# Tile statistics a phase ahead of their transposes, row sums one half step later, inverses widened by TensorE, the value bias on ScalarE

## What is computed

```
x = x + squared(layernorm(x))   # softmax-free: attn = (q k)^2, masked, divided by its row sum + eps
x = x + gated(layernorm(x))     # one shared head of keys and values picked for each token by argmax of a gate
x = x + mqa(layernorm(x))       # 16 heads of queries, one head of keys and values, biases on all products
x = x + gated(layernorm(x))
```

## Time and profile before

| | |
|---|---|
| median of 3 runs | 4368.68 us (4368.31 to 4374.84) |
| the profiled execution | 4371.04 us, of which its span is 4369.3 us |
| TensorE matmul busy | 3769.0 us (86%) |
| GpSimd busy | 2965.8 us (68%) |
| VectorE busy | 1880.1 us (43%) |
| ScalarE busy | 1638.2 us (37%) |
| mean granted TensorE clock | 0.953 |

### The profile page before, as it was taken

How to read it: one execution, slowest core, us unless ns; L and a number is a source line. 1 busy time by engine, 2 the same in 40 slices (tenths; PEclk the granted TensorE clock), 3 DMA queues, 4 the chain that set the end, 5 groups by cost and what they waited for, 6 DMA issues and landing times. The chain is left out here.

```text
span 4369.3 us, 67371 instructions
## 1 busy us (share of the span) xinstructions
PE 3769.0 (86%) x26082; PEld 1520.9 (35%) x26082; DVE 1880.1 (43%) x4874; ACT 1638.2 (37%) x2433; POOL 2965.8 (68%) x2207
## 2 busy tenths in 40 slices
PE   7898998986989899898878878888898898998986
PEld 5343434332433333333333332333333333333332
DVE  1222222222555455455454444444454455555552
ACT  1544544552143333333434333333323333333343
POOL 2888787894076766767777666675565657666687
PEclk8999999998999999999999999999999999999998
DMA  1000100012010100101010010000100101000001
GB/s 68 15 15 22 37 20 30 11 59 73 10 30 1 59 1 23 37 1 40 20 32 28 11 37 13 27 32 15 44 1 15 44 1 59 1 23 27 1 29 40
DMA packets 63385, 115.08 MB, mean 26 GB/s; under 512 B 8673, under 2 KB 9185, under 8 KB 63073
## 3 DMA queue, kind: packets, MB, share of 16 engines
q1 hardware_dynamic: 63072, 110.77, 7.9%
HBM read 77.19 MB, written 33.55 MB: 25 GB/s over the span
## 5 line engine op out<-in xcount | busy, mean ns | idle before, releaser
L866 ACT ACTIVATE probs_soft<-banks 128x1024 f32<-128x1024 f32 (+1 forms) x960 | 848.3, 935 | 1339.8 <-PE banks L1171 1335.4
L774 POOL TENSOR_TENSOR added_soft<-added_soft,probs_soft 128x512 f32<-128x512 f32 (+1 forms) x380 | 1151.8, 3031 | 18.5 <-POOL added_soft L767 3.2
L959 DVE CUSTOM_DVE_ANT_0 banks<-banks,mask 128x128 f32<-128x128 f32 (+3 forms) x1536 | 701.3, 527 | 682.9 <-PE banks L1186 682.9
L954 DVE TENSOR_REDUCE maxima_soft<-banks 128x2 f32<-128x1024 f32 x384 | 452.4, 1221 | 503.3 <-PE banks L1186 503.3
L751 POOL TENSOR_SCALAR_AFFINE_SELECT probs_soft<-probs_soft 128x512 f32<-128x512 f32 x384 | 239.1, 635 | 568.6 <-ACT probs_soft L866 568.3
L1186 PE MATMUL banks<-k_soft,q_soft 32*128 32x512 f32 (+3 forms) x4608 | 508.8, 534 | 64.1 <-ACT probs_soft L866 63.6
L1139 PE MATMUL banks<-wide,xnT_soft 128*128 128x512 f32 x1024 | 500.6, 612 | 19.3 <-DVE picking_soft L938 11.0
L872 ACT ACTIVATE probs_squared<-banks,key_scale_squared 128x512 f32<-128x512 f32 (+3 forms) x768 | 378.9, 588 | 287.3 <-PE banks L1171 282.5
L1171 PE MATMUL banks<-q_soft,k_soft 32*128 32x512 f32 (+3 forms) x4608 | 481.2, 500 | 0.0
L1232 PE MATMUL banks<-probs_soft,v_soft 128*32 128x512 f32 (+3 forms) x4608 | 446.2, 507 | 10.2 <-DVE scaled_out_soft L1083 3.5
L774 POOL TENSOR_TENSOR added_squared<-added_squared,probs_squared 128x512 f32<-128x512 f32 (+1 forms) x124 | 376.9, 3039 | 5.1 <-POOL added_squared L774 1.4
(11 more groups left out here) (152 smaller groups left out, 4271.3 us busy)
## 6 DMA issues: line engine op xcount, KB each, us to landing
tiles_soft<-out SPq DMA_DIRECT2D x96, 256.0 KB, 2.7
rest_soft<-out SPq DMA_DIRECT2D x96, 256.0 KB, 2.9
out<-rest_soft SPq DMA_DIRECT2D x96, 256.0 KB, 2.1
tiles_squared<-in_x SPq DMA_DIRECT2D x32, 256.0 KB, 2.7
rest_squared<-in_x SPq DMA_DIRECT2D x32, 256.0 KB, 2.9
out<-rest_squared SPq DMA_DIRECT2D x32, 256.0 KB, 2.0
wide<-in_gated_wqkvT SPq DMA_DIRECT2D x3, 1024.0 KB, 7.7
raw_wq<-in_squared_wq SPq DMA_DIRECT2D x1, 1024.0 KB, 5.6
```

The costliest lines, as they stand in the source:

```text
L774: ins = pool.tensor_tensor(sums, sums, slot(ph, n)[:, :, col:col + width], ALU.add)
L866: ins = act.activation(slot(ph, n)[:, 2 * a:2 * a + 2, 0:width], score_pair(e, a)[:, :, 0:width], ACT.Exp, scale=SCALE)
L954: ins = dve.reduce_max(m["maxima"][:, ph % 2, 2 * a:2 * a + 2, t, p], score_pair(e, a)[:, :, col:col + width], AX_X)
L959: ins = dve.tensor_tensor_reduce(scores, scores, k["mask"][:, CHUNK - width:CHUNK], 1.0, MASKED, ALU.add, ALU.max, m["maxima"][:, ph % 2, ...
```

## The change

- `norm_events` and `plan`: the `stats` of a stage's first 4 tiles move from the second phase of the stage before (right ahead of the first `ln`) to its first or second phase, sprinkled over that phase's other work (`sprinkled`). The `stats` of tiles 4 to 7 come one `ln` earlier. At most one `ln` goes into a half step, with `due` letting an output that is not due be passed over. The first four `rload` of a stage move to the head of its first phase.
- `SUMS_AT` goes from (15, 9) to (16, 10): `sm` now stands behind the `keys` burst that followed it. `rs` keeps its place, since its distance falls from 2 to 1, and `rw` as well. `nrm` moves with `sm`. The output tiles of the second token half get an earliest half step.
- `widen` goes. `rw` reads the 16 reciprocals directly: 16 matmuls (4 tiles, 4 heads), whose stationary is one column read 32 times, with the identity as moving operand.
- `scaled_out` has 4 buffers in place of 2.
- The value bias is a per-partition bias in ScalarE's copy of `v_parts`; VectorE's addition and the semaphore for it go.

```diff
+SCALED = 4
-SUMS_AT = (15, 9)
+SUMS_AT = (16, 10)
...
         steps.append([("ln", s, t)] + [("load", s, t + TILES)] * (t + TILES < NT))
-        if t >= 2 and t + 2 < NT:
-            steps[-1].append(("stats", s, t + 2))
+        if t and t + 3 < NT:
+            steps[-1].append(("stats", s, t + 3))
...
+def sprinkled(work, some):
+
+    placed, first = list(work), len(work) // 3
+    for n in reversed(range(len(some))):
+        placed.insert(first + (len(work) - first) * n // len(some), some[n])
+    return placed
...
     if kind == "gated":
-        return [(("rs", ph, c), 2)]
+        return [(("rs", ph, c), 1)]
     if kind == "mqa":
-        return [(("rs", ph, c), 2), (("widen", ph, c), 3), (("rw", ph, c), 4)]
+        return [(("rs", ph, c), 1), (("rw", ph, c), 3)]
...
+    if event[0] == "out" and event[2] >= TPC:
+        return SUMS_AT[1] + 4
...
+def due(queue, n):
+
+    for x, (e, first, _) in enumerate(queue):
+        if first <= n:
+            return x
+        if "out" not in (e[0], e[1][0] if e[0] == "more" else ""):
+            return None
+    return None
...
+        head = ([("rload", s - 1, t) for t in range(TILES)] * (s > 0) + head[0], head[1])
...
-            work = [(head[0], 1), (parted(own[0]), HALVES - 2), (mixed(parted(outs[:half]), parted(own[1]), kinds), 2 * HALVES - 2)]
+            work = [(head[0], 1), (sprinkled(parted(own[0]), head[1]), HALVES - 2), (mixed(parted(outs[:half]), parted(own[1]), kinds), 2 * HALVES - 2)]
...
-        work += [(head[1], 2 * HALVES - 2), (parted(merged), 2 * HALVES + 6), (parted(later + first), (3 if kinds[s + 1:s + 2] != ["squared"] else NG) * HALVES - 2),
+        work += [(parted(merged), 2 * HALVES + 6), (parted(later + first), (3 if kinds[s + 1:s + 2] != ["squared"] else NG) * HALVES - 2),
...
-                elif u == "widen":
-                    wait_free(pool, ("rs", *e[1:]))
-                    if place[e]:
-                        wait_work(pool, ("rw", *order["widen"][place[e] - 1][1:]))
-                    pool.tensor_copy(m["wide_inverse"][:], m["few_inverse"][:, :, :, None].broadcast_to([P, TPC, HG, D]))\
-                        .then_inc(sg.widened, 1)
...
-                    take_out(e, m["v_parts"][:, e[2]], work[:, bank(e), :])
+                    take_out(e, m["v_parts"][:, e[2]], work[:, bank(e), :], weights["mqa"]["bv"][:, 0:1])
...
-                        if n >= 2:
-                            dve.wait_ge(sg.summed, n - 1)
+                        if n >= SCALED:
+                            dve.wait_ge(sg.summed, n - SCALED + 1)
...
-                    pe.wait_ge(sg.widened, place["widen", ph, c] + 1)
+                    need(("rs", ph, c))
                     for t in range(TPC):
-                        ins = pe.transpose(tile_of(out, t), m["wide_inverse"][:, t].rearrange("p i d -> p (i d)"), k["ident"][:])
+                        for i in range(HG):
+                            ins = pe.matmul(tile_of(out[D * i:D * i + D, :], t), m["few_inverse"][:, t, i:i + 1].broadcast_to([P, D]), k["ident"][:],
+                                            start=True, stop=True)
```

More of the change, by code:

```diff
@@ L318, in plan @@
         if s:
-            outs = [("rload", s - 1, t) for t in range(TILES)] + [e for t in range(NT) for e in
-                                                                 [("out", s - 1, t)] + [("rload", s - 1, t + TILES)] * (t + TILES < NT)]
+            outs = [e for t in range(NT) for e in [("out", s - 1, t)] + [("rload", s - 1, t + TILES)] * (t + TILES < NT)]
         half = next((n for n, e in enumerate(outs) if e == ("out", s - 1, TPC)), 0)
@@ L342, in plan @@
             own = [features(4 * s + 2), features(4 * s + 3)]
-            work = [(head[0], 1), (mixed(parted(outs[:half]), parted(own[0]), kinds), 2 * HALVES - 2), (parted(own[1]), 3 * HALVES - 2)]
+            work = [(head[0], 1), (sprinkled(mixed(parted(outs[:half]), parted(own[0]), kinds), head[1]), 2 * HALVES - 2), (parted(own[1]), 3 * HALVES - 2)]
             if s == stages - 1:
@@ L587, in act_program @@
     order = {name: [e for e in events if e[0] == name] for name in
-             ("load", "rload", "stats", "out", "mxr", "split", "krep", "vst", "ksq", "qsq", "kvar", "nrm", "rs", "widen", "rw", "gate")}
+             ("load", "rload", "stats", "out", "mxr", "split", "krep", "vst", "ksq", "qsq", "kvar", "nrm", "rs", "rw", "gate")}
     order["picks"] = [e for e in events if e[0] in ("kall", "vall")]
@@ L830, in _ @@
                         pool.wait_ge(sg.rest_in[t % TILES], loads)
-                        pool.tensor_tensor(x, x, m["scaled_out"][:, n % 2, :], ALU.add).then_inc(sg.summed, 1)
+                        pool.tensor_tensor(x, x, m["scaled_out"][:, n % SCALED, :], ALU.add).then_inc(sg.summed, 1)
                 elif u == "rload" and kind_of(e[1]) == "mqa":
@@ L1023, in _ @@
                     ins.then_inc(sg.work_free[bank(e)], 1)
-                    wait_free(dve, e)
-                    dve.tensor_tensor(out, out, weights["mqa"]["bv"][:, None, :].broadcast_to([P, TPC, D]), ALU.add)\
-                        .then_inc(sg.biased_values, 1)
                 elif u == "v2":
@@ L1065, in _ @@
                         if n:
-                            dve.wait_ge(sg.widened, n)
+                            wait_work(dve, order["rw"][n - 1])
                         dve.reciprocal(m["few_inverse"][:], columns).then_inc(sg.work_free[bank(e)], 1)
@@ L1221, in _ @@
                         else:
-                            pe.wait_ge(sg.biased_values, place["vst", s, NC - 1] + 1)
+                            for half in range(NC):
+                                need(("vst", s, half))
                     if not soft:
```

26 lines of the change are left out of this document (14 added, 12 removed).

## The result

The changed kernel takes 4149.66 us (median of 4 runs, 4142.34 to 4152.43) against 4368.57 us for the kernel before, measured beside it. The medians differ by 219 us. The forecast was 4147 us, in a range of 4085 to 4250.

What follows compares the result with a forecast made beforehand. TensorE's work plus 600 us without a matmul bounds it. 4371.0 - 110 (tiles) - 53 (inverses) - 55 (sums) - 50 (clock) + 26 (inverse matmuls) + 20 (collisions) = 4149, so 4147 as median; 8-in-10 range 4085 to 4250.

Steps and rivals of the forecast that it cites:

- What bounds it: Whole kernel: time is TensorE's own work plus its waits, 600 us without a matmul.
- Tiles: TensorE's waits for GpSimd's normalized tiles: first four normalized a phase earlier, gain 110 of 120.1 us.
- The worry: Tiles 4 to 7: load to stats becomes one ln shorter, so 10 us of the gain is left out.
- Inverses: TensorE's waits at rw for widened inverses: 56.8 us becomes 4, gain 53; the 16 matmuls cost 26 us.
- Sums: Row sums waiting for ScalarE's copy of a value part: gain 57.9 us, less 3; counted as 55.
- Clock: Half-clock stretches at tile and inverse waits: 59 us comes back, 50 taken; mean clock to about 0.975.
- Collisions: Moved work on VectorE and GpSimd, and TensorE arriving earlier at exponentials and maxima: nothing to 60 us, 20 taken.
- The bound for being wrong: TensorE's waits for exponentials and maxima: forecast is wrong if they grow by more than 60 us.
- Array drains: Rival: sums between score bursts change the array's shape twice more each, costing 35 us: 4182; chance 0.12.
- Handed over: Rival: half of tile and inverse waits return at other releasers, collisions 30 us larger: 4284; 4215 to 4350, chance 0.17.
- Serial inverses: Rival: the 32 records at rw don't overlap, 0.194 us each, 147 us more than counted: 4294; chance 0.04.
- VectorE's queue: Rival: earlier stats of tiles 4 to 7 hold up maxima, 4.5 us per tile, slower at 4399; chance 0.03.

Runs made afterwards that it cites:

- run with the late tiles back: Changed kernel with only the statistics of tiles 4 to 7 back one step later: 4170.83 us, ratio 0.9544.
- sums alone: Kernel before with only the row sums moved to (16, 10) and widening one step behind rs: 4317.01 us, ratio 0.9880.
- sums undone: Changed kernel with the row sums back at the half steps (15, 9): 4202.73 us, ratio 0.9608.
- inverses alone: Kernel before with only the inverses read directly by 16 matmuls, without widen: 4301.72 us, ratio 0.9845.
- two buffers: Changed kernel with 2 buffers for scaled_out in place of 4: 4148.56 us, ratio 0.9488.
- two buffers, inverses undone: Changed kernel with 2 scaled_out buffers and with widen and the 4 transposes per inverse put back: 4194.87 us, ratio 0.9593.
- tiles alone: Changed kernel with row sums and widen as before and two scaled_out buffers, leaving the tiles' part and value bias: 4255.30 us, ratio 0.9735.
- tiles undone: Changed kernel with the statistics of all tiles back where they were: 4255.24 us, ratio 0.9734.
- doubled run: Changed kernel with the 16 matmuls that read the inverses issued twice, same result written again: 4173.88 us, ratio 0.9546.

## Why the prediction held, step by step

**What bounds it.** The reading that the time is TensorE's work plus its waits held: 195.8 of the 218.6 us came from time without a matmul. By the forecast's own terms that was 110 + 53 + 55 - 20 = 198. The matmuls were to lose 50 - 26 = 24 us, and lost 22.8.

**Tiles.** Forecast 110, of 120.1 us to be had. The wait itself fell by 153.9 - 39.3 = 114.6 us, since only 5.8 us and not 10 were left outside the openings. Undoing the part costs 106 us and having it alone saves 114, both with what it does to the clock. The worry was right in kind, that the later tiles would take something back, and VectorE's wait for tiles did grow, from 40.0 to 50.1 us. The changed kernel's two groups of statistics:

```profile
L993 DVE BATCH_NORM_STATS2 stats_soft<-tiles_soft 128x6 f32<-128x512 f32 x96 | 65.5, 683 | 38.0 <-DMA tiles_soft<-out 38.0
L993 DVE BATCH_NORM_STATS2 stats_squared<-tiles_squared 128x6 f32<-128x512 f32 x32 | 21.9, 685 | 12.1 <-DMA tiles_squared<-in_x 12.1
```

The forecast would be wrong "if VectorE waits for tiles by more than 40 us"; since 40.0 us were there already, this is read as growth, and 10 came. The run with the late tiles back shows that they were not on TensorE's path.

**Inverses.** The gain in waits was right, 52.0 us for a forecast of 53. The cost was the term that was mis-sized: 26 us by 0.05 us per record, from the nearest row of the same shape. Measured were 0.034 us per record, and 0.024 to 0.027 for the second set of them. Against the transposes that is 34.6 - 24.8 = 9.8 us. But the transposes stood behind long waits: 10.3 of their 24.8 us lie in stretches at half clock, and none of the 34.6. At full clock they would have been an estimated 24.8 - 10.3 / 2 = 19.6 us, and the replacement costs 15.0. The forecast had this part of the clock's gain twice, in the 24.8 and in the 59 us of its clock term. The nearest row had 8 records. Of the 0.4 us of so short a group, 273 ns are the length of a single record. In 32 records in a row (1.08 us at 2581.76) each one's share is smaller.

**Sums.** Forecast 55 us. The sums had 57.9 us of waits for a copy of `y`. They have none now, and 2.0 us for other banks (L1213). Undone and alone, the move is worth 53 us each. What was to be late next, the copy of the sums behind two exponentials, is there with 10.2 us in 25 waits of L1323. It was not foreseen that the gated division would then be late for the bank: 17.5 + 11.3 us at L1152 and L1348. The timeline of the changed kernel about 1585 us has such a case:

```profile
1584.66 0.19 DVE L984 TENSOR_REDUCE minus_max_soft<-maxima_soft 128x16 f32<-128x32 f32 x1
1584.77 0.25 DVE L1074 RECIPROCAL inverse_soft<-banks 128x16 f32<-128x16 f32 x1
...
1585.07 1.12 PE L1152 MATMUL banks<-wide,xnT_soft 128*128 128x512 f32 x2 [2.15 <-DVE inverse_soft L1074]
```

The reciprocal, 0.25 us long, stands in VectorE's queue behind a burst's maxima and their reduction, and the projection that wants its bank waits 2.15 us. The 17.5 us are not all new, for they stand in part where another wait of VectorE was. The groups by form show the idle time before these projections in the kernel before:

```profile
L1139 PE MATMUL banks<-wide,xnT_soft 128*128 128x512 f32 x1024 | 500.6, 612 | 19.3 <-DVE picking_soft L938 11.0 <-DVE few_inverse_soft L1067 2.9 <-ACT shift_soft L849 2.7
```

In the changed kernel the idle time of this group (L1152) is 26.6 us, with 17.5 for `inverse_soft` and 2.2 for `picking_soft`. That of the transposes of `y` (L1348) is 33.8 us after 23.6. So they have 7.3 and 10.2 us more, together 17.5 and not 29. The smaller waits for exponentials, 48.3 after 63.6 us, make up for most of that.

**Clock.** Forecast 50 us and a clock of 0.975; 0.972 came. Summed over the stretches that the trace records at half clock, TensorE was busy in them for 272.0 us before and 171.6 us after. Half of the difference, 50 us, is what the clock gave, if work at half clock takes twice as long. The rule of the Trainium skill, page "TensorE: Matmul & The Clock Gate", section "What's actually happening", that the throttled state is the default and activity releases it, agrees with the half-clock time going from 411 to 232 us as the waits went.

The matmuls lost only 22.8 us, so something made them longer by 27.4. To see what, take from TensorE's busy time half of what lies in half-clock stretches. This estimate of the busy time at full clock can be compared between runs:

| | busy | of it at half clock | at full clock, estimated |
|---|---|---|---|
| before | 3769.0 | 272.0 | 3633.0 |
| changed | 3746.2 | 171.6 | 3660.4 |
| sums alone | 3774.4 | 268.6 | 3640.1 |
| sums undone | 3735.8 | 165.9 | 3652.9 |
| inverses alone | 3753.1 | 207.5 | 3649.4 |
| two buffers | 3731.8 | 142.1 | 3660.8 |
| two buffers, inverses undone | 3738.9 | 189.1 | 3644.4 |
| tiles alone | 3748.9 | 225.7 | 3636.1 |
| tiles undone | 3774.6 | 234.5 | 3657.4 |

Alone and undone agree: the inverses add 16 us (15.0 of them the replacement itself), the later sums 7 to 8, the tiles' part 3, which makes up all but 1 us of the 27.4. The forecast had 26 us for the first and nothing for the other two. That 24 us were forecast and 22.8 came is therefore in part luck: the 10 us too many for the inverses stand for 10 us at the sums and the tiles that were not foreseen. Of the sums' part, 3 us are in the projections of L1145 and 1.4 in those of L1152, by the same estimate. Why these matmuls take longer is open.

**Collisions.** Forecast 20 us. The waits that the change aims at fell by 114.6 + 52.0 + 55.9 = 222.5 us, and the time without a matmul by 195.8, so 27 us came back elsewhere. The largest are 17.5 us ahead of the two lines that wait for the bank of the gated division, 10.0 ahead of `av` of the squared kind (28.2 after 18.2, its masks) and 5.5 ahead of `rs` (12.3 after 6.8); the smaller waits for exponentials go against them. The bound for being wrong, 60 us more at exponentials and maxima, is far off: 103.0 us after 117.8, with both rows of the maxima, of which the forecast counted one.

**The rivals.** Array drains would have made 4182. The trace has next to no sign of them. Moving the sums gains 53 us of the 57.9 that they waited. By the estimate at full clock the sums of the changed kernel take 136.4 us after 135.4 with the sums undone, and the score bursts between which they now stand have not grown (keys 632.8 after 632.9, rows 493.6 after 493.7). Even the 7 to 8 us of all longer matmuls would be a fifth of the 35. The rule of the Trainium skill, page "TensorEngine Tiling (Array Packing)", section "Key Properties", that a change of mode drains TensorE is neither proved nor refuted as such; if there is a drain, its cost here is far below the 35 us. Handed over, 4284: of 222.5 us 27 came back, an eighth and not half. Serial inverses, 4294: out by the doubled run. VectorE's queue, 4399: out by the run with the late tiles back.

## What to carry to other kernels

When an in-order engine stands between a producer and the engine that bounds the kernel, look at what is ahead of the short instruction in its queue: moving the instruction up by a whole phase, or past the queue altogether, gives back the wait itself and, where the waits are long, the clock behind them. Price a replacement by a row with as many instructions in a run as it will have, since the share of one falls as the run grows, and look at which clock the replaced work had, or the clock's gain is counted twice. Before a step is moved by a half step to remove a wait, ask which bank it takes and gives back at its new place; here the next wait was for a bank twice.

## What was not expected of the hardware

A second set of 1024 records of 128 x 128 with 32 columns cost 24 us, 0.024 us each, though the records are 274 ns long: they overlap about tenfold (1024 x 0.274 = 281 us in 27.9).

Waits of 0.8 us (77 of them, undone sums) left the mean clock at 0.972, while 20 more tile waits (40 against 20, tiles undone), of up to 10.4 us, took it to 0.961.

The times of one kernel vary with its clock: the fastest of the changed kernel's four runs, 4142.34 us, has a mean clock of 0.974, the slowest, 4152.43, 0.972. Two and four buffers of `scaled_out` gave 4148.56 and 4149.66 us as medians, but their profiled executions have clocks of 0.975 and 0.972. Busy time on the page of the one with two buffers:

```profile
PE 3731.8 (90%) x26978; PEld 1503.6 (36%) x26978; DVE 1897.9 (46%) x4866; ACT 1627.5 (39%) x2433; POOL 2948.3 (71%) x2176
```

Its time without a matmul, 4139.6 - 3731.8 = 407.8 us, is 3 us more than with four. The 11 us between the spans are therefore in the length of the matmuls (3731.8 against 3746.2). At full clock, by the estimate above, the two differ by 0.4 us (3660.8 and 3660.4). A difference of 11 us between two profiles says nothing about an edit as long as the clock is in it.
